# Second cross attention of a perceiver kernel: maxima in a bank of their own, product jobs cut around them, splits behind subtractions, three value tiles moved to their own batch

## What is computed

```python
q = (x @ Wq.T).reshape(B, N, H, D)
k = (y @ Wk.T).reshape(B, L, H, D)
v = (y @ Wv.T).reshape(B, L, H, D)
attn = jnp.einsum('bnhd,blhd->bhnl', q, k)
attn = jax.nn.softmax(SCALE * attn, axis=-1)
out = jnp.einsum('bhnl,blhd->bnhd', attn, v).reshape(B, N, C)
```

## Time and profile before

| | us |
|---|---|
| median of 3 runs | 1368.89 |
| lowest and highest | 1365.0, 1373.93 |
| the profiled execution | 1376.89 |
| its span, first to last instruction | 1375.2 |
| TensorE busy | 1227.7 (89%) |
| VectorE busy | 616.3 (45%) |
| ScalarE busy | 433.8 (32%) |
| GpSimd busy | 70.4 (5%) |

### The profile page before, as it was taken

The page is one execution under the profiler, slowest core; times in us unless marked ns, Lnnn a source line. Parts: engine busy times, 40 slices in busy tenths (PEclk is TensorE's granted clock), DMA queues, the critical chain, the costliest instruction groups (busy, mean ns, idle before and its releaser), DMA issues.

```text
span 1375.2 us, 34061 instructions
## 1 busy us (share of the span) xinstructions
PE 1227.7 (89%) x15423; PEld 924.7 (67%) x15424; DVE 616.3 (45%) x985; ACT 433.8 (32%) x822; POOL 70.4 (5%) x47
## 2 busy tenths in 40 slices
PE   7789888887999999999999999999999999756886
PEld 3334433685887887887887887787787788444773
DVE  2011387544224444444453454455445444544276
ACT  1010252232323343343334324334333333112332
POOL 0000000140000000000000000000000000701022
PEclk9899989899999999999999999999999999855999
DMA  9989850531020000010011010001001001300000
GB/s 355 380 354 389 306 209 28 218 113 51 16 79 20 21 33 32 17 52 32 17 53 33 17 52 32 17 21 64 17 21 62 18 21 35 129 2 1 16 2 31
DMA packets 38875, 115.67 MB, mean 84 GB/s; under 512 B 2504, under 2 KB 3016, under 8 KB 34640
## 3 DMA queue, kind: packets, MB, share of 16 engines
q1 hardware_dynamic: 38736, 113.50, 22.9%
HBM read 112.44 MB, written 1.05 MB: 83 GB/s over the span
## 4 chain that ended last, share of the span: by engine, by line
PE 70%; DVE 14%; issue 5%; SPq 5%; DMA 3%; ACT 3%; POOL 0%; DVEq 0%; ACTq 0%
PE SB L346 40%; PE SB L1052 7%; PE SB L337 5%; PE SC L1022 4%; SPq L501 4%; DVE LN L1331 4%; PE SB L1034 2%; DVE low L1316 2%; DMA R<-in_ctx_t 2%; PE SB L861 2%; DMA R<-in_ctx 1%; PE SB L929 1%; PE SB L330 1%; PE SC L837 1%; DVE Z L1347 1%
## 5 line engine op out<-in xcount | busy, mean ns | idle before, releaser
L346 PE MATMUL SB<-high,whigh 128*128 128x512 f32 (+2 forms) x512 | 186.6, 365 | 13.9 <-DVE low L1316 10.8
L1536 ACT COPY R<-SB 64x512 f32<-64x512 f32 (+1 forms) x240 | 118.5, 494 | 222.3 <-PE SB L346 220.2
L1331 DVE TENSOR_REDUCE LN<-SC 128x64 f32<-128x768 f32 x128 | 116.4, 951 | 152.4 <-PE SC L1022 152.4
L346 PE MATMUL SB<-high,wlow 128*128 128x512 f32 (+2 forms) x512 | 179.9, 351 | 0.0
L346 PE MATMUL SB<-low,whigh 128*128 128x512 f32 (+2 forms) x512 | 179.5, 351 | 0.0
L346 PE MATMUL SB<-whigh,high 128*128 128x512 f32 (+1 forms) x416 | 168.9, 406 | 0.0
L1347 DVE TENSOR_TENSOR Z<-SC,LN 128x768 f32<-128x768 f32 x128 | 116.6, 952 | 116.6 <-ACT LN L1562 116.6
L346 PE MATMUL SB<-whigh,low 128*128 128x512 f32 (+1 forms) x416 | 164.1, 395 | 0.0
L346 PE MATMUL SB<-wlow,high 128*128 128x512 f32 (+1 forms) x416 | 163.8, 394 | 0.0
L1566 ACT ACTIVATE Z<-Z 128x768 f32<-128x768 f32 (+1 forms) x192 | 120.9, 662 | 65.6 <-DVE Z L1347 64.4
L1052 PEld LDWEIGHTS SB<-R,Z 128*64 128x64 f32 (+1 forms) x3328 | 109.4, 145 | 17.0 <-issue 11.7
(11 more groups left out here) (213 smaller groups left out, 1394.5 us busy)
## 6 DMA issues: line engine op xcount, KB each, us to landing
R<-in_ctx_t SPq DMA_DIRECT2D x32, 1024.0 KB, 8.4
R<-in_ctx SPq DMA_DIRECT2D x8, 3072.0 KB
R<-in_ctx_t SPq DMA_DIRECT2D x16, 644.0 KB, 6.7
R<-in_f SPq DMA_DIRECT2D x4, 2048.0 KB, 15.8
R<-in_f SPq DMA_DIRECT2D x1, 8192.0 KB, 25.4
R<-in_ctx_t SPq DMA_DIRECT2D x12, 512.0 KB, 4.2
R<-in_Wk SPq DMA_DIRECT2D x3, 1024.0 KB, 10.1
R<-in_Wv SPq DMA_DIRECT2D x3, 1024.0 KB, 13.2
```

The lines of the kernel that those rows point to most:

```text
L346: last = pe.matmul(out_, lhs[a][:, k, :], rhs[b][:, k, :], start=k == 0 and i == 0, stop=k == NC - 1 and i == 2)
L1331: inc(dve.tensor_reduce(tops[:, r * T:(r + 1) * T], sc_head[:, :, r, 0:6 * T].rearrange("p g (a q) -> p q g a", q=T), AX.XY, ALU.max), "ha ...
L1536: last = act.copy(keys[nu][64 * half:64 * half + 64, pairs, first * P:first * P + full], src[:, :, 0:full])
```

## The change

The list of steps is built by time instead of counts. `fill(us)` takes projection jobs until the given time is used up; where a job does not fit it is cut: a step `p` does its first matmuls, the rest follows in the next fill. The scores are followed by 3.2 us of fill, b by 5.5 us (4.6 in pair 0, 5.2 in pair 7). `split` puts an h that is among the next four jobs right behind b. Transposed maxima (m), their broadcast (b) and the transposed output (c) go to bank 2, with semaphores of their own; the ring for k, v, w and y has two banks (`RING4 = 2`). The value tiles 10 to 12 (`w`, LATE4) leave the projections ahead of their batch and are computed in the batch's own attention, in pair 0. In LAST4 (`filled_out=False`) the outputs o stand right behind the scores of the next pair, ahead of m. Worked out from the functions, the new BATCH4 reads (the number behind p is how many of the job's matmuls are then done):

and the new LAST4 `p(w10,6) s0 w10 p(w11,8) m0 w11 b0 w12 y0 | s1 o0 y1 y2 m1 b1 | s2 o1 m2 b2 | ... | s7 o6 m7 b7 o7 c`. FIRST4 ends with k33. The diff, without the places that only follow from this:

```diff
@@ -101,35 +102,65 @@
     return jobs
-def attention(jobs):
-    jobs = list(jobs)
-    def take(n):
-        taken = []
-        while n and jobs:
-            taken.append(jobs.pop(0))
-            n -= taken[-1][0] != "h"
-        return taken
-    order = []
+def attention(jobs, filled_out=True):
+    jobs, order, begun = list(jobs), [], 0
+    def split():
+        for job in jobs[:4]:
+            if job[0] == "h":
+                order.append(job)
+                jobs.remove(job)
+    def fill(us):
+        nonlocal begun
+        while us > 0 and jobs:
+            kind, x = job = jobs[0]
+            if kind in "kvw":
+                count = 12 * len(x[1]) if kind == "k" else 12
+                each = piece_n(x[0], 1) / 512 * 0.232 if kind == "k" else 0.232
+                if begun + math.ceil(us / each) < count:
+                    begun += math.ceil(us / each)
+                    order.append(("p", (job, begun)))
+                    return
+                us -= (count - begun) * each
+            elif kind != "h":
+                us -= 2.8
+            order.append(jobs.pop(0))
+            begun = 0
+    fill(1.2)
     for pr in range(HP):
-        order += [("s", pr)] + take(1) + [("m", pr)]
-        if pr:
-            order += [("o", pr - 1)]
-        order += [("b", pr)] + take(2 + (pr in (0, 3)))
-    return order + [("o", HP - 1)] + take(1) + [("c", 0)] + jobs
-FIRST4 = [("h", 0), ("q", 0)] + projections()
-BATCH4 = [("h", 0)] + attention(projections())
-LAST4 = attention([("-", 0)] * 3 + [("y", 0), ("-", 0), ("-", 0), ("y", 1), ("-", 0), ("-", 0), ("y", 2)])
-RING4 = 3
+        order.append(("s", pr))
+        if pr and not filled_out:
+            order.append(("o", pr - 1))
+        fill(3.2)
+        order.append(("m", pr))
+        if pr and filled_out:
+            order.append(("o", pr - 1))
+        else:
+            fill(0.9)
+        order.append(("b", pr))
+        split()
+        fill(5.2 if pr == HP - 1 else 5.5 if pr else 4.6)
+    order.append(("o", HP - 1))
+    fill(2.0)
+    return order + [("c", 0)] + jobs
+LATE4 = [("w", t) for t in piece_tiles(KC - 1)]
+EARLY4 = projections()[:-len(LATE4)]
+FIRST4 = [("h", 0), ("q", 0)] + EARLY4
+BATCH4 = [("h", 0)] + attention(LATE4 + EARLY4)
+LAST4 = attention(LATE4 + [("y", 0), ("y", 1), ("y", 2)], False)
+RING4 = 2
 def numbered(steps, first=0):
-    jobs = [x for x in steps if x[0] not in "sohq-"]
+    jobs = [x for x in steps if x[0] not in "sohq-mbpc"]
     return {x: ((n + first) % RING4, (n + first) // RING4) for n, x in enumerate(jobs)}
...
@@ -550,9 +580,12 @@
             def projected(b, c):
-                steps = FIRST4 if isinstance(b, int) and b == 0 else BATCH4
-                at, before = at4(steps, b - 1)
-                n, k = at["v", piece_tiles(c)[-1]]
+                if c == KC - 1:
+                    at, before = at4(BATCH4, b)
+                    n, k = at[LATE4[-1]]
+                else:
+                    at, before = at4(FIRST4 if isinstance(b, int) and b == 0 else BATCH4, b - 1)
+                    n, k = at["v", piece_tiles(c)[-1]]
                 sp.wait_ge(sem(f"full4_{n}"), before + k + 1)
             def load_batch(b):
@@ -636,8 +669,9 @@
             at, before = at4(LAST4, B - 1)
             pool.wait_ge(sem("qb"), B)
-            for n in range(RING4):
-                pool.wait_ge(sem(f"full4_{n}"), before)
+            for late in LATE4[-RING4:]:
+                n, k = at[late]
+                pool.wait_ge(sem(f"full4_{n}"), before + k + 1)
             inc(pool.memset(qb5, 0.0), "zero5")
             pool.wait_ge(sem("zero5"), 1)
             for w in range(3):
...
+                begun = {}
+                def some(job, n):
+                    (kind, x), first = job, begun.get(job, 0)
+                    c, ecs = x if kind == "k" else (piece_of(x), (0,))
+                    if first == 0:
+                        if kind == "k" and ecs[0] == 0:
+                            pe.wait_ge(sem("split"), KC * nxt + c + 1)
+                        bank4(job)
+                    begun[job], bk = n, BK[at[job][0]]
+                    for i, ec in enumerate(ecs):
+                        within = range(max(first - 12 * i, 0), min(n - 12 * i, 12))
+                        if within and kind == "k":
+                            m = piece_n(c, 1)
+                            last = three_products(bk[:, i * m:(i + 1) * m], 0, slice(ec * P, (ec + 1) * P), c,
+                                                  slice(0, m), True, within)
+                        elif within:
+                            m, at_ = min(P, MP - x * P), (x - PIECE_TILE[c]) * P
+                            last = three_products(bk[0:m, :], 1, slice(0, D), c, slice(at_, at_ + m), False, within)
+                    return last
                 for kind, x in steps:
                     job = kind, x
-                    if kind == "k":
-                        c, ecs = x
-                        n = piece_n(c, 1)
-                        if ecs[0] == 0:
-                            pe.wait_ge(sem("split"), KC * nxt + c + 1)
-                        bk = bank4(job)
-                        for i, ec in enumerate(ecs):
-                            last = three_products(bk[:, i * n:(i + 1) * n], 0, slice(ec * P, (ec + 1) * P), c,
-                                                  slice(0, n), True)
-                        done4(job, last)
-                    elif kind == "v":
-                        n, c = min(P, MP - x * P), piece_of(x)
-                        bk, first = bank4(job), (x - PIECE_TILE[c]) * P
-                        last = three_products(bk[0:n, :], 1, slice(0, D), c, slice(first, first + n), False)
-                        done4(job, last)
+                    if kind == "p":
+                        some(*x)
+                    elif kind == "k":
+                        done4(job, some(job, 12 * len(x[1])))
+                    elif kind in "vw":
+                        done4(job, some(job, 12))
                     elif kind == "s":
...
                     elif kind == "m":
-                        bk = bank4(job)
+                        if x == 0:
+                            pe.wait_ge(sem("ot4"), b + 1)
                         pe.wait_ge(sem("tops4"), 8 * b + x + 1)
-                        done4(job, pe.transpose(bk[:, 0:P], tops, ident[:, :]))
+                        inc(pe.transpose(BK[2][:, 0:P], tops, ident[:, :]), "turned4")
                     elif kind == "b":
-                        bk = bank4(job)
-                        n, k = at["m", x]
-                        pe.wait_ge(sem(f"read4_{n}"), before + k + 2)
-                        done4(job, pe.matmul(bk[:, 0:P], mx[:, x:x + 1].to_broadcast([P, P]), ident[:, :],
-                                             start=True, stop=True))
+                        pe.wait_ge(sem("mx4"), 8 * b + x + 1)
+                        inc(pe.matmul(BK[2][:, 0:P], mx[:, x:x + 1].to_broadcast([P, P]), ident[:, :],
+                                      start=True, stop=True), "spread4")
                     elif kind == "o":
                         if x == 0:
                             pe.wait_ge(sem("ones4"), 2)
                             pe.wait_ge(sem("o4_read"), b + 1)
-                            for n in range(RING4):
-                                pe.wait_ge(sem(f"read4_{n}"), before + 1)
+                            for late in LATE4[-RING4:]:
+                                n, k = at[late]
+                                pe.wait_ge(sem(f"read4_{n}"), before + k + 2)
...
                     elif kind == "c":
                         pe.wait_ge(sem("o4_read"), b + 2)
-                        bk = bank4(job)
                         for k in range(2):
-                            last = pe.transpose(bk[:, k * P:(k + 1) * P], on4[:, k * P:(k + 1) * P], ident[:, :])
-                        done4(job, last)
+                            last = pe.transpose(BK[2][:, k * P:(k + 1) * P], on4[:, k * P:(k + 1) * P], ident[:, :])
+                        inc(last, "turned_out4")
                     elif kind == "y":
...
                         copied((kind, x), by_head4[nu][0:n, x, :, 0:HD],
                                lambda bk: bk[0:n, :].rearrange("p (h d) -> p h d", d=HD))
+                    elif kind == "w":
+                        n = tile_keys(x)
+                        copied((kind, x), by_head4[u][0:n, x, :, 0:HD], lambda bk: bk[0:n, :].rearrange("p (h d) -> p h d", d=HD))
                     elif kind == "h":
                         split_low(x)
                     elif kind == "q":
...
                             "tops4")
                     elif kind == "m":
-                        n, k = at[kind, x]
-                        dve.wait_ge(sem(f"full4_{n}"), before + k + 1)
-                        inc(dve.reduce_max(mx[:, x:x + 1], BK[n][:, 0:P], AX.X), f"read4_{n}")
```

(35 more changed lines are left out.)

## The result

The changed kernel takes 1420.31 us (median of 4 runs, 1413.3 to 1426.43) against 1368.27 us before: 1.0355 times as long, 95% interval 1.0316 to 1.0393, +52 us. Forecast were 1406.9 us, slower, in a range of 1372 to 1425.

| stretch | before, us | after, us | difference |
|---|---|---|---|
| up to FIRST4's first product | 337.2 | 333.8 | -3.4 (outside the change) |
| FIRST4 to the first scores | 71.3 | 65.5 | -5.9 |
| seven turns of BATCH4, first scores to first scores | 761.1 | 823.8 | +62.7 |
| last batch, first scores to the end of its outputs | 89.9 | 86.1 | -3.8 |
| the rest | 115.6 | 115.2 | -0.4 |

A forecast was written before the change was run, and what follows sets the result against it. TensorE was taken as the bound, idle 5.0 us a turn. The terms -35.0 + 75.6 - 7.8 + 15.5 - 6.7 - 3.6 gave +38.0 us, so 1406.9 us against the median, range 1372 to 1425.

The forecast's parts named there:

- Removed stalls: In each BATCH4 turn, TensorE's old waits for splits, column maxima and a bank go: -5.0 us a turn, -35.0 over seven.
- all four rows: TensorE's four kinds of wait in six turns of the old kernel, 25.3 us over 42 waits, all predicted to go.
- the estimate for late ends: Listed ends lie behind the true ones: about 0.12 us a wait, 5 us in 42 waits, added to TensorE's idle time.
- The ring of two: Product jobs wait for ScalarE to release key-job banks after b: pairs 1, 4, 6, 7 stall 3.4, 1.1, 1.8, 3.4 us.
- The end of a turn: After the last outputs, o7, no job is left to cover the normalisation, so c waits: +0.8 us a turn.
- The clock: In the turns, half clock at the head goes, -7.8 us; half clock after the new 3.4 us stalls comes, +15.5 us.
- my rate of 5 in 7: Share of the long stalls, two a turn, taken to bring the lower clock, each costing 1.55 us.
- Its 6 us more: If every recurring wait throttled TensorE each time, as the skill says, the total would be 6 us higher.
- Three value tiles: Before the first batch, 36 products leave the stretch, -8.4 us; less a bank wait and an uncovered split, net -6.7.
- the last batch: LAST4 pairs, with products and outputs moved, sum to 86.3 us instead of 89.9: -3.6 us.
- 12 us less at full clock: Bound for the last batch: at full clock throughout, it would take some 12 us less again.
- The faster one: ScalarE's readout keeps up with two banks, leaving the removals and the 0.8: -47.5 us, 1321 us; chance 0.12.

The follow-up runs named there:

- unrolled: The changed kernel with the hardware loop over turns 2 to 7 written out on TensorE, VectorE and ScalarE; 1407.31 us, 1.0279 of the kernel before.
- queries_early: The changed kernel, but ScalarE copies the next batch's queries right after the scores of pair 7, not behind its exponentials; 1397.46 us.
- exp_unrolled_warm: exp_unrolled plus needless float32 products in the last batch where TensorE waits, behind b of pairs 2 to 6 and behind output groups; 1317.65 us.
- exp_behind_keys: The changed kernel, but ScalarE reads out the key job begun before b ahead of that b's three exponentials; 1341.01 us.
- exp_unrolled: The changed kernel with both edits of exp_behind_keys and unrolled: key job read ahead of the exponentials, turns 2 to 7 written out; 1332.19 us.
- fillers: The changed kernel plus 31 needless 512-column products per turn, placed where TensorE waits ahead of k03, v5, v9 and k33; 1404.16 us.

## Why the prediction was right, point by point

**Removed stalls (-5.0 a turn).** Right: all four rows are gone. The idle time, by the rows, was 4.3; the 0.7 more is the estimate for late ends, which no run checks.

**The ring of two (+10.0 a turn).** The mechanism and the four places are right. By the rows it is 47.1 / 6 = 7.9 us. The waits of pairs 1 and 7 were given 3.4 each and measured 2.9 at most; ends listed a little late account for a part of it, and a job at half clock ahead of a wait eats into it.

**The end of a turn (+0.8).** Right for c: 4.6 / 6. But the step stopped there: it named the queue that drains at c, and not what stands behind c, the jump of the loop. That was +1.2 a turn in the mean of idle time alone, in two turns of six. Here "no job is left" had a second consequence that the prediction missed.

**The clock (+15.5 against -7.8).** This is the term that was mis-sized. Per turn, the change cost 117.7 - 108.6 = 9.1 us; idle time rose by 9.8 - 4.3 = 5.5; the other 3.6 are the same products at the lower clock. Predicted were 10.8 - 5.0 = 5.8 for idle time, which holds in sum (bank waits too high, the jump left out), and (15.5 - 7.8) / 7 = 1.1 for the clock. I had priced each long stall like the one of the earlier trace rows, one short stretch worth 1.55 us, five times in seven. The trace after has 71.7 us at the lower level in six turns, 12 a turn. The lower clock came with 11 of the 12 long waits instead of 5 in 7, and it lasted longer: 30.7 us in sum behind pair 1 and 41.0 around the end of the turn, where k33, c and, in two turns, the jump leave three idle pieces close together. That their closeness makes it longer is argued; pair 1's single wait has nearly as much of it. How often it comes is not fixed by the wait either: the same 2.9 us of pair 1 are followed by it in six turns of six here, in four in `unrolled` and in three in `queries_early`. The rule of the Trainium skill (TensorE: Matmul & The Clock Gate, HAM oscillation), that a wait that recurs in each turn throttles the engine each time, was nearer here than my rate of 5 in 7 (11 of 12 long waits), and further off in `queries_early` and `unrolled`. Its 6 us more would still have been too few, because the size was off as well as the number. For the seven turns 48.3 us were predicted and 62.7 measured, 14 more. Of these, the clock gives 2.5 x 7 = 18, the two jumps in six turns 7, the old waits, smaller than thought, 0.7 x 7 = 5, and the bank waits, 2.1 a turn too high, take 15 off again. That the total came as near as 14 us is in part luck: errors of 30 us in one direction met one of 15 in the other.

**Three value tiles (-6.7) and the last batch (-3.6).** -5.9 and -3.8. The late pair was put at 9.2 us and is 9.1 (1260.85 to 1269.95 in the changed kernel's timeline):

```profile
1260.85 0.48 PE L1061 MATMUL SC<-LN,R 32*65 32x64 f32 x4 [2.41 <-DVE Z L1396]
...
1269.95 0.48 PE L1061 MATMUL SC<-LN,R 32*65 32x64 f32 x4 [2.41 <-DVE Z L1396]
```

The bound "12 us less at full clock" was not reached; `exp_unrolled_warm` came nearest, with 8.4 us in the stage.

**The rivals.** The faster one, 1321 us if the readout kept up, is what `exp_behind_keys` (1341) and `exp_unrolled` (1332) made true in kind: their gain on the kernel before is 29 and 39 us where this rival had 47.5, and it did turn on the one place named, who stands ahead of the copy in ScalarE's queue. The Trainium skill's rule of rotating banks (Perfetto Trace Analysis, Matmuls) holds there; in the changed kernel the jobs rotate through the same two banks, and the copy does not overlap in time (6.6 us behind b).

## What to carry to other kernels

Before a ring of buffers is made shorter, write down for each job when the engine that reads it comes to it in its own queue, not how long the copy takes: here a copy of 1.2 us was done 6.6 us behind b. If a stall appears, look at the reader's order first; a copy moved into a gap ahead of an activation was worth 79 us where the whole change was worth -52. On a kernel bound by TensorE, price idle time twice, once as time and once as the clock that follows. Here 10.2 us at the lower clock made a turn 4.2 us longer. And do not take one rate for how often it follows: the same wait was followed by it in three to six turns of six.

## What the hardware showed beyond what was expected

- Filling waits with useless products makes a kernel faster: 16 us with 217 of them in the turns, and 8.4 us in the last batch, where the granted clock went from 0.66 to 0.92.
- A jump back of a hardware loop costs TensorE some 3.5 us (3.2 to 5.0 in these traces) where only c's two transposes stand directly ahead of it; written out, the loop has no such wait, and no other in its place.
- With `fillers` there were four waits without a releaser, 11.3 us in sum, two of them in the middle of a job right behind the jump (1.95 us, one product after the first). An instruction block is moved at 741.9 us, ahead of the end of one of them (744.06); what they are stays open.
